# Layer 1 of a two-layer model: scales, shifts, queries and output gate folded into factors that GpSimd makes

## The reference, cut to what matters

```
mem = scan over time of a * mem + b                  # a gated recurrence
out = ln(mem) * mn_g + mn_b                          # over each of 16 heads of 16 channels
out = out * q                                        # q = l2-normalised queries
o   = ln(out) * gn_g + gn_b                          # again by heads
y   = (o * sigmoid(xc @ og_w.T + og_b)) @ Wo.T       # output gate, output product
x   = x + y + ffn(x_normed)
```

## Time and profile before

| | |
|---|---|
| median of 3 runs | 849.26 us (848.54 to 850.39) |
| profiled execution: own time | 849.49 us |
| its span | 847.5 us |
| TensorE, matmuls busy | 742.0 us, 88% of the span |
| VectorE busy | 633.5 us, 75% |
| ScalarE busy | 468.4 us, 55% |
| GpSimd busy | 423.2 us, 50% |
| granted TensorE clock, mean | 0.949 |

### The profile page before, as it was taken

The page is one execution under the profiler, slowest core; times in us unless marked ns, Lnnn a source line. Parts: engine busy times, 40 slices in busy tenths (PEclk is TensorE's granted clock), DMA queues, the critical chain, the costliest instruction groups (busy, mean ns, idle before and its releaser), DMA issues. The chain is left out here.

```text
span 847.5 us, 15157 instructions
## 1 busy us (share of the span) xinstructions
PE 742.0 (88%) x5602; PEld 638.1 (75%) x5602; DVE 633.5 (75%) x1099; ACT 468.4 (55%) x746; POOL 423.2 (50%) x369
## 2 busy tenths in 40 slices
PE   3368799999999999999999999999779797988773
PEld 2256678888888888888888888888567686877662
DVE  6999877788777686777778777674373998988966
ACT  4246645755655664665566565567656454664411
POOL 2344454354355667658535435436436373763831
PEclk9579999999999999999999999999889999999985
DMA  5111121111011010110100000021100000000000
GB/s 157 28 39 39 39 77 46 45 40 45 3 33 40 21 52 21 39 46 20 28 21 3 21 3 20 21 77 40 52 1 0 1 1 26 1 26 1 1 26 25
DMA packets 22108, 25.89 MB, mean 31 GB/s; under 512 B 4498, under 2 KB 17170, under 8 KB 22036
## 3 DMA queue, kind: packets, MB, share of 16 engines
q1 hardware_dynamic: 22036, 24.93, 10.4%
HBM read 14.83 MB, written 3.28 MB: 21 GB/s over the span
## 5 line engine op out<-in xcount | busy, mean ns | idle before, releaser
L652 DVE TENSOR_REDUCE neg_max<-s_pair 128x4 f32<-128x1024 f32 x127 | 155.0, 1221 | 75.5 <-PE s_pair L866 75.3
L474 ACT ACTIVATE probs<-t_pair 128x1024 f32<-128x1024 f32 x128 | 131.3, 1025 | 135.9 <-PE t_pair L891 135.6
L371 POOL TENSOR_TENSOR hid<-g,hid 128x512 f32<-128x512 f32 x64 | 82.1, 1283 | 177.7 <-DVE g L763 144.6
L365 POOL TENSOR_TENSOR hid_lo<-hid,hid_hi 128x512 fp32r<-128x512 f32 x64 | 85.5, 1336 | 82.7 <-ACT hid_hi L497 82.6
L866 PE MATMUL s_pair<-K,Q 96*128 96x256 f32 x508 | 84.8, 290 | 16.1 <-DVE neg_max L652 9.8
L866 PEld LDWEIGHTS s_pair<-K,Q 96*128 96x128 f32 x508 | 75.5, 194 | 24.5 <-issue 8.1
L891 PE MATMUL t_pair<-Q,K 104*128 104x512 f32 x256 | 85.6, 416 | 0.3 <-DMA Q<-max_parts 0.3
L933 PE MATMUL down<-hi,hid_hi 128*128 128x256 f32 x256 | 83.9, 328 | 0.8 <-POOL hid_lo L365 0.8
L906 PE MATMUL misc<-probs,V 128*32 128x256 f32 x1024 | 69.4, 389 | 4.0 <-DVE kc L608 2.5
L933 PE MATMUL down<-lo,hid_hi 128*128 128x256 f32 x256 | 71.5, 279 | 0.0
L933 PE MATMUL down<-hi,hid_lo 128*128 128x256 f32 x256 | 71.2, 278 | 0.0
(11 more groups left out here) (258 smaller groups left out, 1962.9 us busy)
## 6 DMA issues: line engine op xcount, KB each, us to landing
stage<-in_ternary SPq DMA_DIRECT2D x18, 256.0 KB, 2.8
Q<-q_hi SPq DMA_DIRECT2D x64, 64.0 KB, 2.0
stage<-in_scales SPq DMA_DIRECT2D x8, 384.0 KB, 3.3
X<-in_x SPq DMA_DIRECT2D x8, 256.0 KB, 4.4
Q<-q_lo SPq DMA_DIRECT2D x32, 64.0 KB, 2.0
Q<-max_parts SPq DMA_DIRECT2D x128, 4.0 KB
out<-X SPq DMA_DIRECT2D x8, 256.0 KB, 2.3
signs<-w_stage SPq DMA_DIRECT2D x9, 128.0 KB, 1.8
```

Source lines behind the costliest of these rows:

```text
L365: pool.tensor_tensor(hid_lo[:, m % 2, :, :].rearrange("p a n -> p (a n)"), hid[:, m % 2, :], hid_hi[:, m % 2, :, :].rearrange("p a n -> p ...
L371: pool.tensor_tensor(hid[:, m % 2, :], g[:, m % 2, :], hid[:, m % 2, :], ALU.mult).then_inc(S["hid_done"], 1)
L474: act.activation(probs[:, u % 2, th, :], t_pair[:], ACT.Exp, scale=SCALE).then_inc(S["probs_done"], 1)
L652: dve.tensor_reduce(neg_max[:, u % 2, 4 * jp:4 * jp + 4], score_banks(u, jp)[:].rearrange("p (s n) -> p s n", n=SEQ), AX_X, ALU.max, negat ...
```

## The change

Before, scale and shift were applied after each root, three full operations for each half. After, the products that don't need the root are made ahead of it: GpSimd makes `q_kept * mn_b` (into `o`) and `q_kept * mn_g` (in place) for both halves at the head of its turn, and `gate * gn_b` (into `q_kept`) and `gate * gn_g` (in place) behind `hidden_low(2)`; it multiplies the centered `o` by the latter. VectorE multiplies the centered memory by `q_kept * mn_g` ahead of the root. Behind each root two full operations for each half are left, both on VectorE: times the root, plus the shift product. `queries_kept` moves behind `output_high` on ScalarE, and in the last turn the FFN's sum (`mlp_added`) moves behind `output_applied`.

The diff, cut to what matters:

```diff
-        def memory_scaled(engine, late, b):
...
-        def gated(engine, late, b):
...
+                def queries_weighted():
+                    wait = waiter(pool, late)
+                    wait("q_kept", 1)
+                    wait("o_turned", 0)
...
+                    for b in range(BPG):
+                        inc(pool.tensor_tensor(heads(o[:, pair(b), :]), heads(q_kept[:, pair(b), :]), mn_b, ALU.mult), "mq_done")
+                    for b in range(BPG):
+                        wait("mq_done", b + 1)
+                        inc(pool.tensor_tensor(heads(q_kept[:, pair(b), :]), heads(q_kept[:, pair(b), :]), mn_g, ALU.mult), "mq_done")
+
+                def gates_weighted():
+                    wait = waiter(pool, late)
+                    wait("mw_done", BPG)
+                    wait("gates_done", TPG)
+                    for b in range(BPG):
+                        inc(pool.tensor_tensor(q_kept[:, pair(b), :], gates[:, 1 + late % 2, pair(b), :], gn_b2, ALU.mult), "gw_done")
+                    for b in range(BPG):
+                        g = gates[:, 1 + late % 2, pair(b), :]
+                        wait("gw_done", b + 1)
+                        inc(pool.tensor_tensor(g, g, gn_g2, ALU.mult), "gw_done")
+
+                def output_weighted(b):
+                    wait = waiter(pool, late)
+                    wait("cen_sq", b + 1)
+                    wait("gw_done", BPG + b + 1)
+                    inc(pool.tensor_tensor(o[:, pair(b), :], o[:, pair(b), :], gates[:, 1 + late % 2, pair(b), :], ALU.mult), "xg_done")
...
-                memory_scaled(pool, late, 1)
+                queries_weighted()
                 if early is not None:
                     hidden_low(pool, early, 1)
                     convolved()
                     hidden_low(pool, early, 2)
+                gates_weighted()
+                if early is not None:
                     values(pool, early, 0)
+                output_weighted(0)
+                if early is not None:
                     hidden_low(pool, early, 3)
+                output_weighted(1)
+                if early is not None:
                     hidden_low(pool, early, 4)
                     through_input_gate(pool, early, 0)
-                gated(pool, late, 0)
-                if early is not None:
                     hidden_low(pool, early, 5)
                     through_input_gate(pool, early, 1)
...
                 if early is not None:
-                    queries_kept()
                     hidden_high(5)
                 for b in halves:
                     output_high(b)
+                if early is not None:
+                    queries_kept()
                 if ahead is not None:
                     first_tap(ahead)
...
                     for b in range(BPG):
                         wait("mem_sq", b + 1)
                         inc(dve.tensor_reduce(sm[:, b, :], osq[:, b, :].rearrange("p (h d) -> p h d", d=L1_DH), AX_X, ALU.add), "sm_done")
+                        wait("mq_done", BPG + b + 1)
+                        y = turned(banks[4 + b][:])
+                        inc(dve.tensor_tensor(y, y, q_kept[:, pair(b), :], ALU.mult), "mw_done")
...
                     for b in range(BPG):
                         y = turned(banks[4 + b][:])
-                        inc(dve.tensor_tensor(heads(o[:, pair(b), :] if b else y), heads(y), each(sm[:, b, :]), ALU.mult), "mn_done")
+                        inc(dve.tensor_tensor(heads(y), heads(y), each(sm[:, b, :]), ALU.mult), "mn_done")
+                    for b in range(BPG):
+                        wait("mn_done", b + 1)
+                        inc(dve.tensor_tensor(o[:, pair(b), :], turned(banks[4 + b][:]), o[:, pair(b), :], ALU.add), f"op_done{b}")
...
-                    for b in range(BPG):
-                        y = turned(banks[5][:]) if b else o[:, pair(b), :]
+                    for b in halves:
+                        y = turned(banks[4 + b][:])
+                        wait("xg_done", b + 1)
                         inc(dve.tensor_tensor(heads(y), heads(o[:, pair(b), :]), each(s2[:, b, :]), ALU.mult), "on_done")
+                    for n, b in enumerate(halves):
+                        wait("on_done", n + 1)
+                        inc(dve.tensor_tensor(o[:, pair(b), :], turned(banks[4 + b][:]), q_kept[:, pair(b), :], ALU.add), f"o_done{b}")
...
-                memory_scaled(dve, late, 0)
...
-                if early is None:
-                    mlp_added(0)
-                    mlp_added(1)
                 output_normed()
                 if ahead is not None:
                     xn_low(dve, ahead, 0)
                 output_applied()
-                gated(dve, late, 1)
                 if early is not None:
                     hidden(5)
+                else:
+                    mlp_added(0)
+                    mlp_added(1)
```

More of the change, by code:

```diff
@@ L1038, in layer1 @@
                    b_turned=BPG, scan_done=BPG, mem_centered=BPG, mem_sq=BPG, sm_done=BPG, rm_done=1, mn_done=BPG,
-                   op_link0=2, op_link1=2, op_done0=1, op_done1=1, so_done=BPG, cen_done=BPG, cen_sq=BPG, s2_done=BPG,
-                   ro_done=1, on_done=BPG, o_link0=2, o_link1=2, o_done0=1, o_done1=1,
+                   mq_done=4, mw_done=BPG, op_done0=1, op_done1=1, so_done=BPG, cen_done=BPG, cen_sq=BPG, s2_done=BPG,
+                   ro_done=1, on_done=BPG, gw_done=4, xg_done=BPG, o_done0=1, o_done1=1,
                    o_turned=BPG, o_hi_done=BPG, o_lo_done=BPG, y_done=BPG, res_done=BPG,
@@ L1157, in through_input_gate @@
             inc(engine.tensor_tensor(vn[:, pair(b), :], qk[:, 1, pair(b), :], gates[:, 0, pair(b), :], ALU.mult), f"b_done{b}")
-        def memory_scaled(engine, late, b):
[L1160 to L1167, removed]
-        def gated(engine, late, b):
-            wait = waiter(engine, late)
-            wait("on_done", b + 1)
-            y = turned(banks[5][:]) if b else o[:, pair(b), :]
[L1173 to L1176, removed]
         @block.sync
@@ L1230, in convolved @@
                         inc(pool.tensor_tensor(xc_lo[:, k, :], cs[:, k, :], xc_hi[:, k, :].bitcast(F32), ALU.subtract), "xc_lo_done")
+                def queries_weighted():
+                    wait = waiter(pool, late)
+                    wait("q_kept", 1)
+                    wait("o_turned", 0)
+                    if late == 0:
+                        pool.wait_ge(once["scaled"], 4)
+                    for b in range(BPG):
[18 more added lines that the diff above has]
+                    inc(pool.tensor_tensor(o[:, pair(b), :], o[:, pair(b), :], gates[:, 1 + late % 2, pair(b), :], ALU.mult), "xg_done")
                 if late is None:
@@ L1366, in queries_kept @@
                     wait("norm_done", 1)
-                    wait("op_done0", 0)
-                    wait("op_done1", 0)
+                    wait("o_done0", 0)
+                    wait("o_done1", 0)
                     wait("ro_done", 0)
@@ L1587, in memory_normed @@
                     wait("rm_done", 1)
-                    wait("o_turned", 0)
+                    wait("mw_done", BPG)
                     for b in range(BPG):
                         y = turned(banks[4 + b][:])
-                        inc(dve.tensor_tensor(heads(o[:, pair(b), :] if b else y), heads(y), each(sm[:, b, :]), ALU.mult), "mn_done")
+                        inc(dve.tensor_tensor(heads(y), heads(y), each(sm[:, b, :]), ALU.mult), "mn_done")
+                    for b in range(BPG):
+                        wait("mn_done", b + 1)
+                        inc(dve.tensor_tensor(o[:, pair(b), :], turned(banks[4 + b][:]), o[:, pair(b), :], ALU.add), f"op_done{b}")
                 def output_centered(b):
@@ L1610, in output_normed @@
                     wait("q_kept", 1)
-                    wait("mlp_done", 1)
+                    if early is not None:
+                        wait("mlp_done", BPG)
                     squared, root = (banks[4][:, n * BPG * PAIR_HEADS:(n + 1) * BPG * PAIR_HEADS] for n in range(2))
@@ L1775, in ffn_down @@
                     if early is not None:
-                        if b == 0:
-                            wait("op_done0", 1)
-                        wait("mn_done", b + 1)
+                        wait(f"op_done{b}", 1)
                     for t in range(2 * b, 2 * b + 2):
```

## The result

After: 868.77 us median of 4 runs (867.72 to 870.00), beside 849.54 for the kernel before on the same chip; ratio 1.0227, 95% interval 1.0207 to 1.0248: slower. Forecast were 868.0, within 853 to 873. The profiled execution took 869.67 us (span 867.9), 0.9 above the median. Of the longer span 0.75 us is there before turn 1 begins: VectorE's instructions around 648 are as long as before and already 0.75 later, ahead of anything that the change touches.

The account below looks back on a forecast made before the run. TensorE is busiest overall, but in layer 1 a chain of waits ending in GpSimd's tail ends a turn. Turns 1 to 4 at +8.1, +7.1, +3.2, +0.5 sum to +18.9 on 849.49: 868 us, range 853 to 873.

Parts of the forecast that it names:

- (a): Turn 2: two `mw` products on VectorE ahead of `hidden(0)` make all that follows later, +1.2 us.
- (b): Turn 2: VectorE operations with two SBUF sources wait in turns with GpSimd's for the port, +5.8 us.
- Rival one: GpSimd gets the port only after a run of VectorE operations, so second neighbours don't wait: 856 us, chance 0.16.
- rival two: The port costs nothing extra, because requests slip into GpSimd's gaps: 846.5 us, chance 0.10.
- (c): Turn 2, behind the output root: four VectorE operations replace the path ending on GpSimd, -2.5 us.
- (d): End of turn 2: `hidden(5)` loses the cover of GpSimd's `gated(0)`, so `output_high` starts later, +0.5 us.
- (e): Turn 2, `output_high` to scan: `queries_kept` delays `first_tap`, and VectorE's tap meets GpSimd's work, +2.1 us.
- The clock: TensorE's clock falling in turn 2 after longer idle time ahead of `ffn_up(1)`: 0 in the sum, up to 1.5 us possible.
- rival four: TensorE's lower clock costs time in turn 2 and again after the longer waits: 871 us, chance 0.05.
- Turn 1: As turn 2, but taps wait for GpSimd's `mq` products, +2.2, and the `queries_kept` delay shrinks by 1.2: +8.1 us.
- Turn 3: No group ahead: less port waiting, no `queries_kept` delay, and `hidden(5)` covered by slow transposes: +3.2 us.
- Turn 4: Memory root's operations wait for GpSimd's gate products, +3.9 us; shorter paths behind both roots offset most: +0.5 us.

Follow-up runs that it names:

- e3: The changed kernel with VectorE's two `mw` products (centered memory times weighted queries) moved behind `hidden(0)`: 864.76 us, ratio 1.0178 to the kernel before.
- e2: The changed kernel with GpSimd's four gate products moved to the head of its turn, ahead of `hidden_low(1)`: 855.80 us, ratio 1.0070 to the kernel before.
- e1: The changed kernel with the first guess of the last turn's memory root in PSUM instead of SBUF: 865.35 us, ratio 1.0181 to the kernel before.
- e5: The changed kernel with e1, e2, e3, `queries_kept` behind `first_tap`, queries' shift products behind the taps, last turn's gate shift products earlier: 844.07 us, ratio 0.9941.
- e7: The kernel before with only the output gate folded, gate products at the head of GpSimd's turn, `queries_kept` behind `first_tap`: 845.50 us, ratio 0.9956.
- e9: The kernel before with only `hidden(0)` moved ahead of the two sums of squares on VectorE: 845.59 us, ratio 0.9953.
- e6: e5 with `hidden(0)` moved ahead of the two sums of squares on VectorE: 841.95 us, ratio 0.9914 to the kernel before.

## Why the prediction was right

By its steps, in turn 2:

- (a) right. `hidden(0)` starts 7.35 after the scan instead of 6.15: +1.2. e3 shows it from the other side.
- (b) right. The eight waits of the timeline above, each against its plain length, are 1.08 + 0.89 + 0.49 + 0.29 + 0.74 + 1.09 + 2.18 = 6.76; less the 1.3 of before, +5.5 against 5.8. e2 took the products away from there and with them most of the waits; e1, at the root of turn 4, took only the operands away and the waits went too, but for one. Rival one (GpSimd only after a run) and rival two (no cost) both fall: the three neighbours at 762.16 and 763.85 wait one GpSimd operation each. The Trainium skill (SBUF — State Buffer, "SBUF: two separate sides") has the lock as one for a whole instruction, taken by VectorE with two SBUF inputs; the trace agrees, 1.77 for 0.69, and adds that the two engines then go by turns.
- (c) right: from the first L1648 to the end of the second add 4.66, less the 2.18 of waits in it 2.5, against 5.2: -2.7 for -2.5.
- (d) right: 1.17 instead of 0.74 from the last add to `output_high`, +0.4 for +0.5.
- (e) right: 7.5 instead of 5.5 from `output_high` to the scan, +2.0 for +2.1.
- **The clock was the mis-sized term.** The sum took 0 and the bound 1.5. Between `hidden(0)` and `hidden(2)` the turn lost 1.6 (9.59 became 11.19), with the chunk at 3.34 instead of 2.12. This window of after holds it:

```profile
727.00:738.00 11.00, 10.53 (x50) 9.01 (x51) 7.34 (x19) 4.63 (x8) 1.30 (x1) 0.84 0.00 1
```

The argument that other work of the turn kept the clock at 1.00 was wrong, since that row is of a turn that idled 2.41 there. What was read as rival four happens in turn 2. That (a)'s delay made the clock fall there is argued and not shown: in e5 and e7 `hidden(0)` starts 6.16 and 6.15 after the scan of turn 2, as early as before, TensorE waits 2.71 and 2.69 for it, and the chunk takes 3.39 and 3.25.

Turn 1: +7.5 for +8.1, with the taps 4.73 long instead of 2.71, +2.0 for +2.2; the port waits came to 5.5 for 5.8 there too, and `output_high` to the scan to +0.8 for +0.9. Between `hidden(0)` and `hidden(2)` it lost 0.3 that the sum did not have. Turn 3: +2.45 for +3.2; its waits came to 0.4 less than the term, and `output_high` to the scan was 0.3 shorter than before.

Turn 4: the memory root took 6.3 as forecast, with a detail wrong: the forecast had the waits begin at the first operation with two SBUF sources (L1500 before, L1515 here), but L1514 ahead of it, with one, waited as well (1.29). The end of the first add behind the output root, the half that TensorE takes first, came 0.59 later after the scan, for the 0.5 of the sum. The other 1.0 of its 1.6 is the clock again: the windows over the output product, of after and of before, whose mean is higher because the clock rose to the full level ahead of the end:

```profile
856.00:865.00 9.00, 7.46 (x32) 6.76 (x32) 4.75 (x8) 1.20 (x2) 0.00 (x0) 0.52 0.09 29
```

```profile
838.00:845.00 7.00, 5.70 (x30) 4.98 (x28) 2.77 (x4) 1.19 (x2) 0.76 (x1) 0.66 0.10 34
```

From VectorE's first `output_low` to the last residual 5.26 became 6.28. Whether less idle time ahead would have kept that clock was not tried.

Also wrong was "GpSimd without a gap from `convolved` to `xn_low`": it idles 3.08 at 769.85, waiting for `hidden_high(5)`. No step of the chain above waits for GpSimd after it. The close total (868.0 for 868.77) owes something to cancellation: 2.6 of clock not counted (1.6 in turn 2, 1.0 in turn 4) and 0.75 ahead of turn 1, against 0.6 and 0.75 too much in turns 1 and 3 and 0.7 in the other terms of turn 2, with an execution 0.9 above its median.

## What to carry to other kernels

Before work is moved to an idle engine, lay it beside what the other engine does in that very stretch: the same four GpSimd products in each of three turns cost 13 us more in one place than in another, and in e5 making GpSimd wait made the turn shorter. An operation's price depends on where its operands lie: beside a busy GpSimd, VectorE's operations with two SBUF sources wait here, and those with one of the two in PSUM do not. When an operation goes ahead of the one that TensorE waits for, look at the clock as well as the delay: in turns 1 and 3 of e9 `hidden(0)` came 1.2 earlier, and the turns were 2.3 and 1.9 shorter. And try a plain change of order by itself before a rewrite is given the credit: in e9 it was worth 0.47%, and the fold with its moves 0.39% on top of it.

## What was not expected of the hardware

In the last turn VectorE's L1514, one SBUF source and an SBUF result, 64 elements, took 1.29 beside GpSimd's products; with a PSUM result, in e1, 0.23. The reductions, with one SBUF source and an SBUF result too, did not wait (0.64 each at 756.33). What sets them apart no run here shows. TensorE's clock did not follow the length of the idle time ahead of a chunk alone. In the rows above the chunk behind `hidden(0)` had the full level after 1.51, 2.00 and 2.41 us and fell to the lower one after 2.69, 3.62 and 3.91. But in turn 1 of e6 it took 2.66 after 2.04 (mean granted clock 0.75), and in turn 3 of e2 it kept the full level after 2.90:

```profile
774.90 2.11 PE L1791 MATMUL lbank<-lo,hi 128*128 128x512 f32 x8 [2.90 <-DVE l_hid L1573]
```

There the clock had fallen one chunk earlier (3.67 long, at 766.55) and was back at the full level before the wait.
